# A decoder layer on one core: the last four rows by order tables of their own, and slot weights worked out in the tile stage

## What is computed

```python
x = x + attention(norm(x))              # 16 heads of 16, rope, causal
x = x + long_conv(norm(x), k, skip, ctx)  # kv = v*ctx, causal convolution, times ctx, summed
h = norm(x)
p = softmax(h @ gate_w.T); top 4 of 16 experts, weights p / sum of the four p
shared = (silu(gate) * up) @ shared_down.T * sigmoid(h @ shared_gate_vec.T)
x = x + shared + sum over the 4 experts of weight * expert(h)
```

## Time and profile before

| | us |
|---|---|
| median of 3 runs | 610.66 (610.11 to 612.71) |
| profiled execution, its own time | 613.6 |
| its span, first to last instruction | 611.8 |
| busy: TensorE | 574.5 (94%) |
| busy: VectorE | 491.7 (80%) |
| busy: ScalarE | 412.1 (67%) |
| busy: GpSimd | 396.5 (65%) |

### The profile page before, as it was taken

One profiled execution on the slowest core, in us unless ns is written; L12 is line 12 of the kernel. 1 busy time (PEld: TensorE's weight loads), 2 busy tenths in 40 slices (PEclk: granted clock), 3 DMA queues, 4 the chain that ended last, 5 costly groups with the idle time before them and its releaser, 6 DMA issues.

```text
span 611.8 us, 18693 instructions
## 1 busy us (share of the span) xinstructions
PE 574.5 (94%) x5883; PEld 465.4 (76%) x5883; DVE 491.7 (80%) x1518; ACT 412.1 (67%) x1060; POOL 396.5 (65%) x439
## 2 busy tenths in 40 slices
PE   7789899999999999999999999988799999999991
PEld 2458779888898898888988988867477777777770
DVE  4557788989989789899887786677677799999992
ACT  3876876878768778787786675733166666666660
POOL 1147758879888888878788887786400355554562
PEclk9998999999999999999999999999999999999997
DMA  8826333243333332433322021011454587888863
GB/s 225 293 80 172 82 118 118 84 131 109 95 137 85 108 116 61 155 80 121 104 72 96 3 87 46 11 44 63 141 144 132 175 233 232 230 244 230 225 175 107
DMA packets 55682, 79.00 MB, mean 129 GB/s; under 512 B 7202, under 2 KB 46370, under 8 KB 55588
## 3 DMA queue, kind: packets, MB, share of 16 engines
q1 hardware_dynamic: 37300, 48.56, 27.0%
q0 software_dynamic: 6912, 18.88, 10.7%
q10 hardware_dynamic: 11376, 10.36, 4.9%
HBM read 44.48 MB, written 33.29 MB: 127 GB/s over the span
## 4 chain that ended last, share of the span: by engine, by line
PE 77%; POOL 7%; issue 6%; DMA 4%; DVE 3%; ACT 3%; POOLq 0%; DVEq 0%; ACTq 0%
PE ps L789 11%; PE ps L664 9%; PE ps L559 7%; PE ps L592 6%; PE ps L490 5%; PE ps L686 5%; PE ps L547 4%; PE ps L612 4%; PE ps L812 4%; PE ps L596 3%; POOL kv_lo L1511 2%; PE ps L801 2%; PE ps L778 2%; DMA toeplitz_lo<-y_slots,slots 2%; PE ps L530 2%
## 5 line engine op out<-in xcount | busy, mean ns | idle before, releaser
L1511 POOL TENSOR_TENSOR kv_lo<-kv,kv_hi 128x512 f16<-128x512 f32 x64 | 80.3, 1255 | 30.6 <-ACT kv_hi L929 30.3
L1582 POOL DMA_INDIRECT toeplitz_lo<-y_slots,slots x44 | 42.7, 970 | 79.8 <-DMA y_slots<-kv 59.7
L789 PE MATMUL ps<-w_gate_up_hi,toeplitz_hi 128*128 x316 | 84.0, 314 | 2.3 <-DVE toeplitz_hi L1419 2.0
L1550 POOL DMA_INDIRECT x_slots<-x_norm,slots x64 | 69.1, 1079 | 18.9 <-issue 14.9
L1499 POOL TENSOR_TENSOR kv<-ctx_t_sb,v_t 128x512 f32<-128x512 f32 x64 | 69.1, 1088 | 15.9 <-ACT v_t L918 15.7
L898 ACT ACTIVATE probs<-ps,row_neg_max 128x128 f32<-128x128 f32 x256 | 71.6, 391 | 0.5 <-DVE row_neg_max L1106 0.3
L559 PEld LDWEIGHTS ps<-v_ones,probs_t 128*128 128x128 f32 x512 | 62.2, 192 | 2.2
L559 PE MATMUL ps<-v_ones,probs_t 128*128 128x17 f32 x512 | 60.7, 256 | 0.0
L592 PE MATMUL ps<-kv_hi,toeplitz_hi 128*128 128x128 f16 x256 | 56.6, 221 | 3.3 <-POOL kv_lo L1511 1.7
L1015 ACT ACTIVATE toeplitz_hi<-ps 128x256 f16<-128x256 f32 x79 | 30.3, 383 | 41.3 <-ACT stage L1034 17.9
L592 PE MATMUL ps<-kv_hi,toeplitz_lo 128*128 128x128 f16 x256 | 56.4, 220 | 0.0
(11 more groups left out here) (228 smaller groups left out, 2075.9 us busy)
## 6 DMA issues: line engine op xcount, KB each, us to landing
stage<-in_w_units SPq DMA_DIRECT2D x36, 512.0 KB, 3.8
x_slots<-zeros SPq DMA_DIRECT2D x15, 512.0 KB
...
```

Source lines behind the costliest of these rows:

```text
L789: last = nc.tensor.matmul(psum[2 + t % 2][:, 0:2 * INTER], bxT[a][t % 2][:, kc, :], egu[b][:, bass.ds(e, 1), kc, :].rearrange("p a n -> p ...
L1511: nc.gpsimd.tensor_tensor(flat(kvh[1][g % 2]), kv[g % 2][:].rearrange("p h j i -> p (h j i)"), flat(kvh[0][g % 2]), ALU.subtract).then_inc ...
L1550: pool.indirect_dma_start(out=xbuf, out_offset=bass.IndirectOffsetOnAxis(ap=slots[:, row, j:j + 1], axis=0), in_=xn[2][row % 2][:], in_off ...
L1582: pool.indirect_dma_start(out=yg[n][j], out_offset=None, in_=ybuf[0:(last_tile(row, j) + 1) * P], in_offset=bass.IndirectOffsetOnAxis(ap=s ...
```

## The change

From step 17 on, all four compute engines leave `ORDER` and walk `DRAIN`, a table for each that names piece and row. In it the pieces of rows 12 to 15 are mixed anew, with row 15's convolution and router ahead of older rows' shared-expert work, and `LATE_BANKS` gives these uses PSUM banks of their own choosing. Row 15's four `kv` products move from GpSimd to VectorE, which reads v straight from PSUM; for this the `t3` transposes now write PSUM in the order that the product reads. Row 15's residual and normalised values get buffers of their own, so that `nm3:15` and `r2:15` need not wait for rows 13's readers. `px` gains one small matmul and `pa` reads its result. The per-row slot weights are gone (`se`, `ss`, `sr`, `cw`, `c1`, `c2`, `c3`); instead keys and router exponentials of all rows are kept, and 28 VectorE operations, seven for each four rows, one a step in steps 2 to 29 of the tile stage, work the weights out. The dummy matmuls ahead of the tiles go from 16 to 4, and `store_shared` of row 15 is issued after the first eight tile loads.

```diff
-LAST = NB + 4
-LAST_FIRST = {
-    "DVE": ("tp", "pk", "mr", "mk", "lm", "cg", "s10", "pf", "pn", "pa", "pm", "pp", "pw", "ky", "k8", "pe", "ix"),
-    "POOL": ("pg", "sct0", "sct1", "sct2", "sct3"),
...
+DRAIN_FROM = NB + 1
+DRAIN = {n: [(p.split(":")[0], int(p.split(":")[1])) for p in pieces.split()] for n, pieces in {
+    "PE": "px:12 ga1:12 v:15 sc01:15 up0:12 sc23:15 up1:12 pt0:15 cv0:14 Th0:12 pt1:15 at0:15 cv1:14 cv2:14 t5:13 "
+        "pt2:15 Th1:12 at1:15 pt3:15 at2:15 at3:15 ro:13 t2:15 cv3:14 wo:15 ga0:13 px:13 dn:12 t3:15 t4:14 ga1:13 "
...
+        "gm0:14 k8:12 pe:12 gm1:14 ix:12 hl0:12 gm2:14 xl:13 sks:14 hl1:12 rcp:15 on:15 tp:13 pk:13 mr:13 mk:13 "
+        "lo2:15 gm3:14 r1:15 st2:15 ag2:15 ve2:15 lm:13 cg:13 pf:13 pn:13 pa:13 pm:13 nr2:15 pp:13 ky:13 k8:13 "
...
+LATE_BANKS = (
+    "cv0:14 xT:13 o2T:14 cv0:15 xT:14 o2T:15 xT:15 up0:15",
+    "cv3:14 vT:15 cv3:15",
...
-        ex = ring("router_exp", 2, [P, EXPERTS])
-        esel = sb("router_sel", [P, EXPERTS])
-        esum = sb("router_sum", [P, 1])
-        erec = sb("router_recip", [P, 1])
-        cwe = ring("expert_weight", 2, [P, EXPERTS])
+        ex = sb("router_exp", [P, NB, EXPERTS])
         cws = ring("shared_weight", 2, [P, 1])
-        key = ring("slot_key", 2, [P, EXPERTS])
+        key = sb("slot_key", [P, NB, EXPERTS])
+        causal_sb = key[:].rearrange("p b e -> p (b e)")[:, 0:P]
         k8 = ring("slot_top", 2, [P, 8])
-        hit = sb("slot_hit", [P, TOP, EXPERTS])
-        hitw = ring("slot_weight_of", 2, [P, TOP, EXPERTS])
...
+        x2_last = st[:, 2752:2752 + E]
+
+        xn3_last = y_sb[0]
+
+        def x2_of(row):
+            return x2[row % 2][:] if row < NB - 1 else x2_last
+
+        def xn3_of(row):
+            return xn[2][row % 2][:] if row < NB - 1 else xn3_last
+
+        hit = sm[0][:].rearrange("p s n -> p (s n)")[:, 0:QUADS * TOP * EXPERTS]
+        picked_ex, wanted = sm[1][:, 0, 0:QUADS * TOP], sm[1][:, 3, 0:QUADS * TOP]
+        ex_sum, ex_recip = sm[1][:, 1, 0:QUADS], sm[1][:, 2, 0:QUADS]
...
-        def bank(use):
-            return psum[HOME[use][0]]
+        LATE = [[(u.split(":")[0], int(u.split(":")[1])) for u in line.split()] for line in LATE_BANKS]
+        LATE_HOME = {use: b for b, line in enumerate(LATE) for use in line}
+        LATE_AFTER = {use: last for line in LATE for last, use in zip(line, line[1:])}
+
+        def bank(use, row=0):
+            return psum[LATE_HOME.get((use, row), HOME[use][0])]
 
         def free(pe, use, row):
-
+            if (use, row) in LATE_AFTER:
+                u, r = LATE_AFTER[use, row]
+                READER[u][0].wait(pe, r, READER[u][1])
+                return
...
-            for s in range(NB + DEPTH):
+            for s in range(DRAIN_FROM):
...
+            for name, row in DRAIN["PE"]:
+                pieces[name](row)
+                if (name, row) in table_after:
+                    table_after[name, row]()
...
-            keep_busy(16, 7)
+            keep_busy(4, 7)
...
+            store_shared(NB - 1)
...
+                nc.tensor.matmul(part(3, 4), share, many(tile_end[:], 1), start=True, stop=True, skip_group_check=True)
...
-                nc.vector.tensor_tensor(ahead[:], newest[row % 2][:], tile_end[:], ALU.subtract).then_inc(page_step.sem, 1)
+                nc.vector.tensor_tensor(ahead[:], newest[row % 2][:], bank("px", row)[:, 3 * EXPERTS:4 * EXPERTS], ALU.subtract)\
+                    .then_inc(page_step.sem, 1)
...
-                nc.scalar.activation(vT[row % 2][:].rearrange("p (h c) i -> p c h i", c=KC),
-                                     bank("vT")[:, 0:E].rearrange("p (c h i) -> p c h i", c=KC, i=SIDE), ACT.Copy)\
+                nc.scalar.activation(vT[row % 2][:].rearrange("p h i -> p (h i)"), bank("vT")[:, 0:E], ACT.Copy)\
...
+            def products_kv(g):
...
+                    vs = bank("vT")[:, 0:E].rearrange("p (h a i) -> p h a i", a=1, i=SIDE)[:, part]
+                    cs = c_sb[row % 2][:, part].rearrange("p h (j a) -> p h j a", a=1)
+                    nc.vector.tensor_tensor(kv[g % 2][:], cs.broadcast_to([P, SIDE, SIDE, SIDE]),
+                                            vs.broadcast_to([P, SIDE, SIDE, SIDE]), ALU.mult).then_inc(kv_ready.sem, 1)
...
-                if row >= 2:
+                if 2 <= row < NB - 1:
                     act.wait_ge(s_sc[row % 2], 64 * (row // 2))
-                xn3_T.wait(act, row - 2)
+                if row < NB - 1:
+                    xn3_T.wait(act, row - 2)
...
+            def weigh(n, k):
+                rows = slice(QUADS * n, QUADS * (n + 1))
+                each = hit.rearrange("p (b j e) -> p b j e", b=QUADS, j=TOP)
+                of = picked_ex.rearrange("p (b j) -> p b j", b=QUADS)
+                if k == 0:
+                    slots_done.wait(dve, NB - 1)
+                    weigh_step.wait(dve, n - 1)
+                else:
+                    weigh_step.wait(dve, n, k)
+                if k == 0:
+                    nc.vector.tensor_scalar(wanted, slots[:, rows].rearrange("p b j -> p (b j)"), 1.0, None, ALU.add)\
+                        .then_inc(weigh_step.sem, 1)
+                elif k == 1:
+                    nc.vector.tensor_tensor(
+                        each, key[:, rows].rearrange("p b (j e) -> p b j e", j=1).broadcast_to([P, QUADS, TOP, EXPERTS]),
+                        wanted.rearrange("p (b j e) -> p b j e", b=QUADS, e=1).broadcast_to([P, QUADS, TOP, EXPERTS]),
+                        ALU.is_equal).then_inc(weigh_step.sem, 1)
+                elif k == 2:
+                    nc.vector.tensor_tensor(each, each, ex[:, rows].rearrange("p b (j e) -> p b j e", j=1)
+                                            .broadcast_to([P, QUADS, TOP, EXPERTS]), ALU.mult).then_inc(weigh_step.sem, 1)
+                elif k == 3:
+                    nc.vector.tensor_reduce(picked_ex, hit.rearrange("p (s e) -> p s e", e=EXPERTS), X, ALU.add)\
+                        .then_inc(weigh_step.sem, 1)
+                elif k == 4:
+                    nc.vector.tensor_reduce(ex_sum, of, X, ALU.add).then_inc(weigh_step.sem, 1)
+                elif k == 5:
+                    nc.vector.reciprocal(ex_recip, ex_sum).then_inc(weigh_step.sem, 1)
+                else:
+                    nc.vector.scalar_tensor_tensor(
+                        out=cw4[:, rows], in0=of, scalar=1.0 / WS, in1=ex_recip.rearrange("p (b j) -> p b j", j=1)
+                        .broadcast_to([P, QUADS, TOP]), op0=ALU.mult, op1=ALU.mult).then_inc(weigh_step.sem, 1)
...
+                if 0 <= s - 2 < 7 * QUADS:
+                    weigh(*divmod(s - 2, 7))
...
-            def weigh_slot(row):
-                hit_step.wait(pool, row, 1)
-                sel_step.wait(pool, row)
-                cw4_done.wait(pool, row - 2)
-                nc.gpsimd.tensor_tensor(hitw[row % 2][:], hit[:], cwe[row % 2][:].rearrange("p (a e) -> p a e", a=1)
...
-                                            in_=xn[2][row % 2][:], in_offset=None).then_inc(s_sc[row % 2], 16)
+                                            in_=xn3_of(row), in_offset=None).then_inc(s_sc[row % 2], 16)
```

165 lines of the change are left out of this document (77 added, 88 removed), and 34 rows, old and new, of tables (DRAIN, ORDER, PREPARE_LO).

## The result

| us | before | after |
|---|---|---|
| median, 22 runs each on one chip | 612.47 | 609.46 |
| ratio after to before, 95% interval | | 0.996 (0.9944 to 0.9975) |
| profiled execution, its own time / span | 613.6 / 611.8 | 609.71 / 607.9 |
| TensorE busy / VectorE busy | 574.5 / 491.7 | 575.1 / 479.1 |
| GpSimd busy | 396.5 | 387.7 |

The change makes the kernel 0.4% faster, about 2.5 us. The kernel before itself is now at 612.47, 1.8 us above the 610.66 that the forecast of 606.5 started from, so the ratio is what to compare. I forecast 4.2 us less; with 2.5 the result lies within the 0.5% that counts as "same", where I gave "faster" 0.72.

A forecast was written before the change was run, and what follows sets the result against it. TensorE bounds the kernel, so other engines matter only where it waits, in the row stage's last steps. -2.6 - 2.9 + 0.4 + 0.9 = -4.2 us: 609.4 from the profiled 613.6, median 606.5, range 602.5 to 609.5.

The forecast's parts named there:

- Dummies, -2.6: Ahead of the tiles: 12 fewer dummy matmuls at 0.216 us each save 2.6 us, if the tile loads are there.
- Six waits, 3.7 us for 6.6, -2.9: Last rows, new order: TensorE's idle time falls from 6.6 us to 3.7 us in six places, saving 2.9 us.
- packing rival: Last rows: the tables pack better than the walk, only the last wait is left, weights hide fully; -7.6, 603.1 us; chance 0.19.
- GpSimd freed by 4.4 us: Row 15's convolution: moving the four products to VectorE frees 4.4 us of GpSimd; r2:15 starts 4.3 us sooner.
- `px`, +0.4: Row stage, on TensorE's path: one more matmul in px, 16 of 0.025 us, costs 0.4 us.
- the slot weights taken out: Row stage: removing the per-row weight operations is worth 0 outside the last steps, as TensorE's full busy time hides them.
- Weights, +0.9 in the tile stage: Tile stage: 28 VectorE operations cost nothing in steps 2 to 22; the fourth group, steps 23 to 29, costs 0.9 us.
- the last steps end no sooner: Last rows: no wait goes and only the dummies are saved; -1.3, 609.4 us; chance 0.04.
- GpSimd slowed: Row 15's convolution: VectorE's products slow all four low halves on GpSimd, ending it 2.6 us later; 609.1 us; chance 0.06.
- VectorE as the bound of the tile stage: Tile stage: uncovered weight operations delay x_lo and TensorE's gate products, all 8.4 us paid; +3.3, 614.0 us; chance 0.05.
- The clock: With dummies gone, late loads leave a hole and TensorE's clock falls to half once, losing 1.65 us; 608.1 us; chance 0.04.
- The marks: Profile signs named beforehand as showing the forecast right, such as last scatter before 430 and first tile turn at 434 to 436.

The follow-up runs named there:

- e5: The changed kernel with 16 dummy matmuls again instead of 4, nothing else; 611.99 us, ratio 0.9984 to the kernel before.
- e4: The kernel before with 4 dummy matmuls instead of 16, nothing else; 613.74 us, ratio 1.0034 to the kernel before.
- e3: The changed kernel without the 28 slot-weight operations, one memset of constant weights in their place; 609.33 us, ratio 0.9962 to the kernel before.
- e6: The changed kernel with row 15's four kv products back on GpSimd, from the vT copy; 613.65 us, ratio 1.0024 to the kernel before.

## Why the prediction was wrong

**Dummies, -2.6.** Right: 3.46 to 0.87, and 3.45 again in e5. So is what I named as the cover: the loads landed in time in the changed kernel, and in e4, where they did not, TensorE waited 2.09 us.

**Six waits, 3.7 us for 6.6, -2.9.** This is the step that failed: the term for the new order measured nothing. TensorE's idle time in the last rows went from 6.58 to 5.98 us (e3), and their length from 55.90 to 55.87. My six places were real, and two of them were smaller than I gave, but four were larger by 0.2 to 0.6 us, and there are three more that I had not seen:

| place | predicted | measured, changed kernel |
|---|---|---|
| `t2:15` | 0.4 | 0.62 |
| `cv0:15`, `cv1:15` | 0.5 | 0.25 and about 0.1 |
| `ro:14` | 0.7 | 0.88 |
| `Th1:13`, `up0:14` together | 0.4 | 0.56 and 0.39 |
| `ro:15` | 0.6 | 0.93 |
| `dn:15` | 1.1 | 1.03 |
| not seen: `t5:14`, `px:15`, `dn:14` | 0 | 0.38, 0.26, 0.37 |
| sum | 3.7 | 5.8 |

I gave the packing rival 0.19 on the ground that my walk rounds delays up. It left them out instead: I stopped at the handovers I had looked for, and took for gains what row 15 won on VectorE and GpSimd (its second residual 39.0 us behind `px:12` before, 35.7 in e3, 3.3 sooner where I said 4.3). The waits account for 0.6 to 0.8 us of gain where I had 2.9; that even this does not show in the length goes with the 0.57 us of busy time named under e3. A row that is earlier is no gain while TensorE has other rows' work to do and waits elsewhere.

**GpSimd freed by 4.4 us.** The size was near enough, since e6 is 3.9 us slower than the changed kernel; but I set it against the old order, which waited for GpSimd 1.3 us in all. The gain was needed to pay for the new order.

**`px`, +0.4.** One more small matmul for each row cannot be told from noise in 600 us; in the last four rows it is 0.1 us. Among profiles without a fall of the clock ahead of `px:12`, the old row stage (e4) reached it at 379.34 us and the new one at 378.97 to 379.84. So neither this matmul, nor the `t3` transposes in another order, nor the slot weights taken out cost or gained anything there that can be told from the spread; for the last two I had put 0.

**Weights, +0.9 in the tile stage.** Wrong, 0 (e3). The group of seven takes 1.9 us (0.42, 0.42, 0.41 and four of 0.17), near my 2.1, and VectorE falls behind as I said; but TensorE's slack against it is larger than the 0.5 us that I allowed.

**The rivals.** Nearest is "the last steps end no sooner", given 0.04, with -2.6 + 0.4 + 0.9; with the weights at zero and `px` below notice it is the measured -2.5. GpSimd slowed: refuted, row 15's four `kv_lo` took 2.27 and 2.26 us in pairs, 1.13 each. Only one of them ran beside one of VectorE's products, the second of the first pair, beside the product of 0.69 us that began at 406.39. GpSimd after, then VectorE:

```profile
404.94 2.27 POOL L1577 TENSOR_TENSOR kv_lo<-kv,kv_hi 128x512 f16<-128x512 f32 x2 [1.22 <-ACT kv_hi L972]
```
```profile
406.39 0.69 DVE L1189 TENSOR_TENSOR kv<-ctx_t_sb,ps 128x512 f32<-128x512 f32 x1
```

The Trainium skill (GPSIMD Engine Reference, the table of its hardware figures) has this contention only for VectorE instructions with two SBUF inputs or in a two-port mode; the products read one operand from PSUM, and the trace agrees as far as that one overlap goes. VectorE as the bound of the tile stage: refuted by e3. The clock: I looked for the fall at the end and argued that waits of 1.18 us had not done it. It came behind one of 0.62, and in half of the profiles only; where it comes it costs 1.07 us by these profiles, and not my 1.65.

**The marks.** Four `kv` products of 0.68 us on VectorE: right. Last scatter before 430: 430.52. First turn 434 to 436: 438.18. Idle 3 to 4 us: 6. Waits in steps 23 to 29: none. The clock at 1.00: not always.
